# Attention row sums in one PSUM row instead of three, in an eight-core layer kernel

## What is computed

```python
xn = _layernorm(x, axis=-1)
x  = x + _L0_attn_ref(xn, w_qkv, w_o) + _L0_ffn_ref(xn, gate, kernel, bias, lora_A, lora_B, ...)

# _L0_attn_ref: 32 query heads, 8 key/value heads, head size 128, 4096 tokens, causal
scores = einsum('bhqd,bhkd->bhqk', q, k) * scale      # q, k after rope
scores = where(causal, scores, finfo.min)
attn   = softmax(scores, axis=-1)
out    = einsum('bhqk,bhkd->bhqd', attn, v)
return einsum('bso,do->bsd', out.reshape(...), w_o)
```

## Time and profile before

| | |
|---|---|
| time, median of 2 runs | 6298.72 us (6204.39 and 6393.04) |
| profiled execution, its own time | 5998.48 us |
| span of its slowest core (core 3) | 5996.9 us |
| spans of the other cores | 5893.5 to 5986.4 us |
| mean granted TensorE clock, by core | 0.857 to 0.864 of full speed |
| TensorE matmuls busy in the span | 4185.3 us (70%) |
| VectorE busy in the span | 1295.2 us (22%) |
| ScalarE busy in the span | 976.6 us (16%) |

### The profile page before, as it was taken

The page is one execution under the profiler, slowest core; times in us unless marked ns, Lnnn a source line. Parts: engine busy times, 40 slices in busy tenths (PEclk is TensorE's granted clock), DMA queues, the critical chain, the costliest instruction groups (busy, mean ns, idle before and its releaser), DMA issues.

```text
span 5996.9 us, 45421 instructions; the slowest of 8 cores (5893.5 to 5996.9 us)
## 1 busy us (share of the span) xinstructions
PE 4185.3 (70%) x16144; PEld 1526.0 (25%) x16144; DVE 1295.2 (22%) x2130; ACT 976.6 (16%) x1041; POOL 556.1 (9%) x866
## 2 busy tenths in 40 slices
PE   2223499499959976666666666666666899567788
PEld 0000244244424421111111111111111344223233
DVE  0444322100112222222222222222222001011122
ACT  2223000000000013333333333333333000000000
POOL 0000000000000011111111111111111000010010
PEclk9666799799979988888888888888888899788899
DMA  9666333433276620000000000000000654465543
GB/s 138 116 115 119 107 95 104 98 98 91 61 124 90 101 42 25 25 25 25 25 23 21 25 25 25 25 24 24 25 23 20 103 99 76 90 114 124 116 99 96
DMA packets 412764, 419.83 MB, mean 70 GB/s; under 512 B 63360, under 2 KB 374912, under 8 KB 412160
## 3 DMA queue, kind: packets, MB, share of 16 engines
q0 software_dynamic: 219712, 249.10, 23.9%
q1 hardware_dynamic: 192832, 167.82, 9.1%
HBM read 495.46 MB, written 83.89 MB: 97 GB/s over the span
## 4 chain that ended last, share of the span: by engine, by line
PE 62%; DMA 11%; DVE 10%; ACT 7%; another core or an unknown queue 5%; issue 3%; DVEq 0%; POOL 0%; ACTq 0%; SPq 0%; POOLq 0%
PE kv_p L86 14%; PE a_rw L81 10%; PE a_av L86 9%; ACT a_p L81 7%; PE q_p L86 7%; PE w_p L86 7%; PE f_p L86 7%; DVE a_rc L81 7%; DMA sc_xkv<-lkv_o 6%; DMA f_at<-sc_at 4%; PE a_s L86 2%; PE a_s L81 2%; DVE lkv_o L81 1%; PE f_pl L86 1%
## 5 line engine op out<-in xcount | busy, mean ns | idle before, releaser
L81 ACT ACTIVATE a_p<-a_s,p_btab 128x1024 bf16<-128x1024 f32 x768 | 814.8, 1111 | 3192.0 <-PE a_s L81 3191.9
L86 PE MATMUL a_av<-a_p,a_v 128*128 128x512 bf16 x1536 | 641.1, 417 | 415.2 <-ACT a_p L81 298.2
L81 PE MATMUL a_rw<-a_p,p_onesb 128*1 128x512 bf16 x1536 | 626.5, 408 | 0.0
L86 PE MATMUL f_p<-f_k,f_x 128*128 128x512 bf16 x2048 | 471.9, 390 | 181.4 <-DVE f_s L81 137.7
L86 PE MATMUL kv_p<-kv_w,kv_x 128*128 128x512 bf16 x1984 | 441.6, 381 | 82.9 <-DMA kv_w<-wvT 82.9
L86 PE MATMUL q_p<-q_x,q_w 128*128 128x512 bf16 x1984 | 441.1, 380 | 71.3 <-DMA q_x<-sc_xkv 71.3
L86 PE MATMUL kv_p<-kv_x,kv_w 128*128 128x512 bf16 x1984 | 440.6, 380 | 66.1 <-DMA kv_x<-sc_xkv 66.1
L86 PE MATMUL w_p<-w_w,p_attn 128*128 128x512 bf16 x1984 | 440.7, 380 | 37.0 <-DMA w_w<-woT 37.0
L81 DVE TENSOR_TENSOR a_p<-a_p,p_cm 128x512 bf16<-128x512 bf16 x256 | 97.5, 422 | 1685.8 <-ACT a_p L81 1685.8
L81 PE MATMUL a_rw<-a_rc,p_onesf 1*128 1x512 f32 x128 | 130.6, 1122 | 417.9 <-DVE a_rc L81 417.9
L86 PEld LDWEIGHTS a_av<-a_p,a_v 128*128 128x128 bf16 x1536 | 148.5, 97 | 908.2 <-issue 908.2
(11 more groups left out here) (96 smaller groups left out, 2363.0 us busy)
## 6 DMA issues: line engine op xcount, KB each, us to landing
kv_x<-sc_xkv SPq DMA_DIRECT2D x16, 4096.0 KB, 17.9
lkv_x<-xTkv POOLq DMA_DIRECT2D x8, 4096.0 KB, 37.8
sc_xkv<-lkv_o SPq DMA_DIRECT2D x256, 128.0 KB, 1.9
q_w<-wqT POOLq DMA_DIRECT2D x16, 2048.0 KB, 16.7
w_w<-woT POOLq DMA_DIRECT2D x8, 4096.0 KB, 27.7
f_k<-kern POOLq DMA_DIRECT2D x8, 4096.0 KB, 30.4
a_k<-sc_k POOLq DMA_DIRECT2D x384, 64.0 KB, 2.1
a_v<-sc_v POOLq DMA_DIRECT2D x192, 128.0 KB, 2.7
```

The costliest lines, as they stand in the source:

```text
L81: getattr(eng, m)(*aa, **kk).then_inc(s, st)
L86: getattr(eng, m)(*aa, **kk)
```

## The change

All row-sum matmuls of a head go to partition 0 of `p_rw[z]`. The `tile_position` argument is gone, and `start` and `stop` are now the same as those of the V matmul next to it. The matmuls themselves, their number and their order stay. At the end of a round the two copies and two additions on VectorE are gone with their waits, and the reciprocal reads `p_rw[z]` in PSUM directly. `rc1` and `rc2` stay allocated.

```diff
-                                            col = kt if kt < 3 else 0
-                                            rw_start = (vi == 0 and kt == col)
-                                            rw_stop = (vi == nv - 1 and
-                                                       kt == (3 if col == 0 else col))
                                             pe.call("matmul", p_av[z][:],
                                                     vb[par][:, kt * 128:(kt + 1) * 128],
                                                     psb[zz][:, t * CH:(t + 1) * CH],
                                                     start=(first and t == 0),
                                                     stop=(last and t == 1),
                                                     inc=False)
-                                            pe.call("matmul",
-                                                    p_rw[z][32 * col:32 * col + 1, :],
+                                            pe.call("matmul", p_rw[z][0:1, :],
                                                     sb_onesb[:, 0:1],
                                                     psb[zz][:, t * CH:(t + 1) * CH],
-                                                    start=rw_start,
-                                                    stop=rw_stop,
-                                                    tile_position=(0, 32 * col))
+                                                    start=(first and t == 0),
+                                                    stop=(last and t == 1))
...
                                 ve.wait(s_pe, rcs_dep)
-                                ve.wait(s_ve, ve.ctr.v)
-                                ve.call("tensor_copy", rc1[0:1, :], p_rw[z][32:33, :])
-                                cc2 = ve.call("tensor_copy", rc2[0:1, :], p_rw[z][64:65, :])
-                                ve.wait(s_ve, cc2)
-                                t1v = ve.call("tensor_add", rcs[0:1, :], p_rw[z][0:1, :],
-                                              rc1[0:1, :])
-                                ve.wait(s_ve, t1v)
-                                t2v = ve.call("tensor_add", rcs[0:1, :], rcs[0:1, :],
-                                              rc2[0:1, :])
-                                ve.wait(s_ve, t2v)
-                                rv = ve.call("reciprocal", rcs[0:1, :], rcs[0:1, :])
+                                rv = ve.call("reciprocal", rcs[0:1, :], p_rw[z][0:1, :])
```

## The result

| | before | after |
|---|---|---|
| median of all runs | 6234.01 us (10 runs) | 5894.25 us (11 runs) |
| lowest run | 5950.77 us | 5746.58 us |
| profiled execution | 5998.48 us | 5767.66 us |
| span, mean of 8 cores | 5941.1 us | 5709.2 us |
| attention, mean of 8 cores | 2493.5 us | 2273.2 us |

The changed kernel takes 0.9655 of the time, 95% interval [0.9563, 0.9747]: 3.45% less.

The account below looks back on a forecast made before the run. TensorE's chain was taken to bound the kernel, waiting 64 times for VectorE's reciprocal. The shorter chain saves 196.5 us, the reciprocal from PSUM, row sums and clock 0: 5998.5 - 196.5 = 5802 us, range 5750 to 6150.

Parts of the forecast that it names:

- Part 1: Round ends: four VectorE instructions fewer per head save 3.07 us each, 6.14 us a round, 196.5 us in all.
- Part 2: Reciprocal reading PSUM instead of SBUF: taken as 0 us more; far bound 0.68 us each, 44 us in all.
- Part 3: Row-sum matmuls all into one row: pitch unchanged, taken as 0 us; upper bound 108 us.
- Rival B: Row sums into one row cost TensorE 108 us, giving 5910 us; chance 0.05.
- Rival E: Row sums without a named position no longer break the matmul stream: 276 us more gained, 5526 us; chance 0.04.
- Part 4: TensorE's clock around round ends: still low and returning as now, taken as 0; bounds 70 us either way.
- A: Nothing of note at round ends: the VectorE chain is covered, time stays 5998 us; chance 0.05.
- C: After each round the clock stays low longer and the kernel is slower, 6152 us with five half-visits per round; chance 0.04.
- D: After each round the clock returns one half-visit earlier, 70 us more gained, 5732 us; chance 0.08.

Follow-up runs that it names:

- experiment 2: Kernel before, row sums still in three rows, but the reciprocal reads row 0 of PSUM directly without copies and additions: ratio 0.9612, attention 2274.1 us.
- experiment 8: Changed kernel with two V products, then two row sums, these at three column positions; reciprocal reads row 0 alone: ratio 0.9159 to before, attention 1998.7 us.

## Why the prediction was right in its mechanism and wrong as a number

**The scale was the step that failed.** The sum was 5998.5 - 196.5 = 5802 us, 3.3% less, and the measured ratio is 3.45% less. But "The point is given on the scale of the profiled execution", while the time shown for the kernel before was the median of two runs, 6298.7. Against that, 5802 reads as 7.9% less, where 3.45% was measured. The sentence "nothing in the profile explains that, and the change doesn't act on it" was true of the offset of 206 and 395 us, and its consequence wasn't drawn: an offset that stays has to be added back to the point, or taken out of both. The runs showed that the offset isn't a constant either. Ten runs of the kernel before go from 5950.77 to 6470.6 us with a median of 6234.01, eleven of the changed kernel from 5746.58 to 6166.75 with a median of 5894.25. So the 6102 that the prediction worked out for the median was too high, and its point of 5802 too low. With a before known only from two runs, 6204 and 6393, the ratio was the sound forecast and a single time was not. The range, 5750 to 6150, held 5894 because it had been stretched for this; that is no merit of the sum. The near agreement of 3.3% and 3.45% is in part luck: the interval, 2.5 to 4.4%, can't tell 196.5 us from the 220.3 that attention shrank by.

**Part 1, the chain: right.** 3.07 us for each head was forecast. The waits fell by 203.0 us on the profiled cores (core 3 before, core 7 after) for 196.5. At the lower clock in both, the piece from the first spreading matmul to the second shrank by 10.29 - 7.10 = 3.19 us. In the kernel before, the product for head 0 in the round of the earlier trace rows is

```profile
4014.66 0.69 DVE L81 COPY a_bc<-a_rw 128x512 f32<-128x512 f32 x1 [2.29 <-PE a_rw L81]
4015.45 0.69 DVE L81 TENSOR_TENSOR p_attn<-a_av,a_bc 128x512 bf16<-128x512 f32 x1
```

and the first copy for head 1 starts 0.80 us behind its start, at 4016.25, when the product has ended. Now the reciprocal starts at 3000.03, 0.61 us behind the start of the product at 2999.42, which lasts 0.69 and so hasn't ended. That is 0.19 us gained with the wait that the change dropped there; 0.07 go back, since `a_bc` is copied 2.22 us behind the spreading matmul instead of 2.15. The remaining 0.12 is what 3.19 has beyond 3.07, and 32 x 0.12 = 4 us. All of it reached the end, as experiment 2 shows by itself.

**Part 2, PSUM: right.** 0 was taken, and the reciprocal went from 3341 to 3340 ns.

**Part 3, row sums in one row: right.** The pitch stayed at 0.31 us, and three rows or one with the same short chain gave 2274.1 and 2273.2 us. Rival B is out. Rival E's cost is real, its condition was not met: the row sums have the form 128*1 with a named position and without, the pitch stayed at 0.31 without one, and a full-width operand (128*128) brought it to 0.21 to 0.22. It was priced at 276 us by the pitch alone; the full-width sums brought 314.5, with a part by the clock. That the positions are worth nothing where a V product stands between two row sums was read from one pitch at all three of them. Experiment 2 confirms it, and in experiment 8 two neighbours at different positions take 0.38 us where they took 0.59 at one. Three neighbours were not measured here.

**Part 4, the clock: its place was missed, its size within the bounds.** Forecast 0, with 70 us either way. "I expect the clock still to be low" failed for the first spreading matmul, which ran at the higher level in 23.8 of 32 rounds (mean of the cores). It takes 0.95 us less from there to the second (32 rounds: 204.6 instead of 32 x 7.10 = 227.2, or 22.6 us). The visits became 6.1 us longer. The argument that 4.62 and 8.25 us of idle time leave the same clock behind them said nothing about 1.55, which was the new one. It was also read from one round in which the clock had fallen before the chain began: the last row sums of the earlier trace rows already take 0.58 us, against 0.38 at the higher clock.

The sum after the fact: 196.5 forecast + 4 (wait) + 23 (clock) + 3 (what the first break gave beyond its half of 196.5: 171.4 - 70.5 = 100.9 instead of 98.2; not taken apart) - 6 (visits) = 220 us, and attention shrank by 220.3.

**Rivals.** A is out by experiment 2, C and D by the visits, which are 6 us longer than the 1895 before, where one half-visit in each round would be 70. For C it was said that "the clock is sensitive to TensorE's breaks", from the one break of the earlier trace rows. The runs show it by the break before the first spreading matmul: none of 256 rounds was at the higher level after one of 4.62 to 5.48 us (before), 190 of 256 after one of 1.40 to 2.34 (after), and with the long chain for head 0 alone none of 256 again. What C made of it did not come: TensorE was at the lower level for 342.5 us of the visits after the change and 333.9 before.

## What to carry to other kernels

Count what one engine's waiting list holds, not what it is busy with: VectorE was busy 22% of the span, and four small instructions of 0.68 us on one row of its data for each head cost 3.45% of the kernel, because TensorE stood behind them 64 times. Alternating narrow and full-width matmuls is itself a cost, 0.1 us each way here. Grouping the narrow ones halves it (151.5 us). Different column positions for neighbours bring another 123, but here they leave the sum in three rows, and the chain that adds these up cost about 219 us (2491.9 against 2273.2). Making the row sums full width was best: 314.5 us, and it also did the spreading. And where two runs of the kernel before lie 3% apart and up to 7% above its profile, forecast a ratio, and say to which time it belongs.

## What the runs showed of the hardware

- A matmul with one output column between full-width ones has a pitch of 0.31 us to each neighbour, a full-width one 0.21 to 0.22. Grouping two by two brings four matmuls from 1.26 to 1.05 us.
- Two neighbouring one-column matmuls over 512 columns take 0.38 us together at different column positions and 0.59 at one.
- After a break of TensorE of 1.4 to 2.3 us the first spreading matmul ran at the higher clock in 190 of 256 rounds, after one of 4.6 to 5.5 us in none of 256. With full-width row sums the break was 2.2 to 2.7 us, and it was 224 of 256.
- VectorE's reciprocal of 512 float32 values takes 3341 ns from SBUF on one partition, 3340 from PSUM, and 3358 on 128 partitions from PSUM.
- Two copies of 1x512 float32 by VectorE take 1.28 us together when both read the same row of PSUM, and 1.40 when they read rows 32 and 64.
